# Attention scores as three products of split queries and keys, and the rotary swap of neighbours done by DMA

## The reference, cut to what matters

```python
q = apply_rope(split_heads(x @ Wq))        # pairs (x1, x2) -> (x1*cos - x2*sin, x1*sin + x2*cos)
k = apply_rope(split_heads(x @ Wk))
v = split_heads(x @ Wv)
sim = einsum('bid,bjd->bij', q, k) * d ** -0.5
sim = where(tril, sim, -inf)
out = einsum('bij,bjd->bid', softmax(sim), v) @ Wo + bo
x = layernorm(x + out)                     # then the experts and a second layernorm
```

## Time and profile before

| | |
|---|---|
| median of 3 runs | 835.21 us (835.08 to 835.27) |
| profiled execution: its span, from the first to the last instruction | 833.1 us |
| what lies around the span, against the median | 2.1 us |
| PE / PEld busy | 813.1 / 587.2 us |
| DVE / ACT / POOL busy | 675.5 / 629.0 / 553.9 us |
| granted TensorE clock, mean | 0.997 |
| units 2 to 61, each | 10.19 us without router work on PE, up to 11.0 us with it |

### The profile page before, as it was taken

The page is one execution under the profiler, slowest core; times in us unless marked ns, Lnnn a source line. Parts: engine busy times, 40 slices in busy tenths (PEclk is TensorE's granted clock), DMA queues, the critical chain, the costliest instruction groups (busy, mean ns, idle before and its releaser), DMA issues.

```text
span 833.1 us, 21102 instructions
## 1 busy us (share of the span) xinstructions
PE 813.1 (98%) x6267; PEld 587.2 (70%) x6267; DVE 675.5 (81%) x2711; ACT 629.0 (76%) x1672; POOL 553.9 (66%) x612
## 2 busy tenths in 40 slices
PE   8999999999999999999999999999999989999995
PEld 4556667666666666666666666666666669999994
DVE  6787798889888988898889988988898866224996
ACT  4677787888788878887888788878887766555576
POOL 5765646456756775667568866675677336899893
PEclk9999999999999999999999999999999999999998
DMA  5111101000100010001000100010012257424434
GB/s 164 33 40 39 52 20 33 8 20 27 53 14 26 27 40 14 26 28 39 15 27 26 39 15 27 26 39 15 14 36 72 71 143 205 131 82 127 128 114 155
DMA packets 55438, 46.09 MB, mean 55 GB/s; under 512 B 6368, under 2 KB 47072, under 8 KB 55328
## 3 DMA queue, kind: packets, MB, share of 16 engines
q1 hardware_dynamic: 50960, 35.90, 15.0%
q0 software_dynamic: 4224, 8.72, 3.1%
q10 hardware_dynamic: 144, 0.13, 0.1%
HBM read 28.39 MB, written 12.14 MB: 49 GB/s over the span
## 4 chain that ended last, share of the span: by engine, by line
PE 94%; DVE 3%; issue 1%; ACT 1%; DMA 1%; POOL 0%; SPq 0%; DVEq 0%
PE TB L1026 18%; PE S_all L979 18%; PE TB L1010 14%; PE S_all L1177 7%; PE AO L1047 7%; PE TB L1190 4%; PE AO L1190 4%; PE AO L906 4%; PE S_all L1010 3%; PE AO L908 3%; PE AO L907 3%; PE AO L968 1%; PE AO L970 1%; PE AO L969 1%; PE AO L903 1%
## 5 line engine op out<-in xcount | busy, mean ns | idle before, releaser
L1295 ACT ACTIVATE Pr_all<-Sm,nmax 128x512 f32<-128x512 f32 (+3 forms) x512 | 279.6, 550 | 0.0
L1504 DVE CUSTOM_DVE_ANT_0 Sm<-S_all,causal 128x512 f32<-128x512 f32 (+3 forms) x512 | 220.2, 487 | 70.9 <-PE S_all L979 70.8
L665 POOL TENSOR_TENSOR shared<-shared,sin_t 128x512 f32<-128x512 f32 x63 | 80.3, 1275 | 172.3 <-DVE shared L1484 172.1
L1307 ACT ACTIVATE PT<-TB 128x1024 f32<-128x1024 f32 x185 | 130.9, 742 | 63.8 <-PE TB L1010 62.8
L979 PE MATMUL S_all<-kT,qT 64*128 64x512 f32 (+3 forms) x1024 | 166.7, 443 | 1.9 <-POOL kT L668 0.9
L1026 PE MATMUL TB<-PT,shared 128*64 128x128 f32 x1008 | 152.3, 441 | 2.3 <-ACT PT L1307 0.3
L1525 DVE SCALAR_TENSOR_TENSOR x_acc<-AO,rinv,x_acc 128x128 f32<-128x128 f32 x504 | 141.7, 344 | 3.5 <-PE AO L1047 1.2
L1010 PEld LDWEIGHTS TB<-ident,Pr_all 128*128 128x128 f32 x1000 | 108.0, 141 | 38.3 <-ACT Pr_all L1295 21.1
L1010 PE MATMUL TB<-ident,Pr_all 128*128 128x128 f32 x1000 | 133.8, 277 | 0.5 <-ACT PT L1307 0.5
L979 PEld LDWEIGHTS S_all<-kT,qT 64*128 64x128 f32 x1024 | 78.9, 187 | 71.2 <-issue 54.4
L1026 PEld LDWEIGHTS TB<-PT,shared 128*64 128x64 f32 x1008 | 60.5, 136 | 52.0 <-issue 32.7
(11 more groups left out here) (320 smaller groups left out, 1423.9 us busy)
## 6 DMA issues: line engine op xcount, KB each, us to landing
wo<-in_wo SPq DMA_DIRECT2D x64, 64.0 KB, 1.8
PT<-yrows SPq DMA_DIRECT2D x7, 512.0 KB
w_tile<-in_wup SPq DMA_DIRECT2D x10, 256.0 KB
xt<-xrows SPq DMA_DIRECT2D x32, 65.0 KB
x_acc<-in_x SPq DMA_DIRECT2D x8, 256.0 KB
wdown<-in_wdown SPq DMA_DIRECT2D x8, 256.0 KB, 3.2
pay<-pay SPq DMA_DIRECT2D x8, 256.0 KB
x_acc<-pay SPq DMA_DIRECT2D x8, 256.0 KB
```

Of the source, the lines that this page charges most:

```text
L665: nc.gpsimd.tensor_tensor(k_rot, k_rot, sin_t[:, :], ALU.mult).then_inc(k_mul, 1)
L1295: nc.scalar.activation(Pr[j][:, 0:n], Sm[j], ACT.Exp, bias=nmax[:, j:j + 1], scale=-1.0, accum_out=rsum[p][:, h * QB + qb:h * QB + qb + 1] ...
L1307: last = nc.scalar.activation(PT[p][:, :, 0:qb + 1, qb * P:qb * P + P], source, ACT.Copy)
L1504: nc.vector.tensor_tensor_reduce(out=Sm[j], in0=SB[2 * (group % 2) + h][:, at:at + n], in1=causal[:, T - n:T], scale=-0.125, scalar=HUGE, ...
```

## The change

Three things change, all in the attention.

- **The rotation.** DVE multiplies the projected k by the cosine table and, as it is, by a sine table whose rows are swapped (`sign[::-1]` in `rope_tables`). The swap of neighbours comes after: two DMAs issued by SP write the odd rows of `k_rot` into the even rows of `kT`, and the even into the odd. POOL then adds `k_cos`. The same for q. Units 0 and 1 (`PLAIN`) swap on DVE with the `stream_shuffle` that all units used.
- **The split.** From unit 2 on, ACT copies `kT` into `k_hi` with rounding to float32r and POOL writes `k_lo = kT - k_hi`; the same for the last 384 queries.
- **The scores.** Query blocks 1 to 3 are each the sum of three float32r products, high*high, high*low and low*high. Block 0 (128 keys) stays one float32 product, and is now ahead of block 2 in its group.

`PT` and `Pr` are packed more closely (`pt_written`, `pt_rows`), which makes room in SBUF; the shapes that are copied stay the same. The experts' part is unchanged.

```diff
+PLAIN = 2
+SWAPPED = 2 * 16
@@ SP, at the end of each unit
+                if u + 2 < UNITS:
+                    swap_k(u + 2, p)
+                    swap_q(u + 2, p)
+            def swap_k(u, p):
+                sp.wait_ge(k_read, u + 1)
+                wait(sp, scored, BLK * (u - 1))
+                sp.dma_start(kT[p][0:P:2, :], k_rot[1:P:2, :]).then_inc(k_swapped, 16)
+                sp.dma_start(kT[p][1:P:2, :], k_rot[0:P:2, :]).then_inc(k_swapped, 16)
+            def swap_q(u, p):
+                sp.wait_ge(q_read, u + 1)
+                sp.dma_start(qT[p][0:P:2, :], q_rot[1:P:2, :]).then_inc(q_swapped, 16)
+                sp.dma_start(qT[p][1:P:2, :], q_rot[0:P:2, :]).then_inc(q_swapped, 16)
@@ POOL
             def rotate_k(u, p):
-                pool.wait_ge(k_read, u + 1)
-                nc.gpsimd.tensor_tensor(k_rot, k_rot, sin_t[:, :], ALU.mult).then_inc(k_mul, 1)
-                wait(pool, scored, BLK * (u - 1))
-                pool.wait_ge(k_mul, u + 1)
-                nc.gpsimd.tensor_tensor(kT[p][:, :], k_cos, k_rot, ALU.add).then_inc(k_ready, 1)
+                pool.wait_ge(k_swapped, SWAPPED * (u + 1))
+                nc.gpsimd.tensor_tensor(kT[p][:, :], k_cos, kT[p][:, :], ALU.add).then_inc(k_ready, 1)
+            def split_k(u, p):
+                pool.wait_ge(qk_high, 2 * (u - PLAIN) + 1)
+                nc.gpsimd.tensor_tensor(k_lo[p][:, :], kT[p][:, :], k_hi[p][:, :], ALU.subtract).then_inc(qk_split, 1)
+            def split_q(u, p):
+                pool.wait_ge(qk_high, 2 * (u - PLAIN) + 2)
+                nc.gpsimd.tensor_tensor(q_lo[p][:, :], qT[p][:, P:T], q_hi[p][:, :], ALU.subtract).then_inc(qk_split, 1)
...
                     rotate_k(u + 2, p)
                     rotate_q(u + 2, p)
+                    split_k(u + 2, p)
+                    split_q(u + 2, p)
@@ PE, score(u, p, group)
+                for qb in sorted(GROUPS[group]):
...
+                    for h in range(2):
+                        nc.tensor.matmul(banks[h], q_hi[p][halves[h], rows], k_hi[p][halves[h], 0:n], start=True, stop=False)
+                    for h in range(2):
+                        nc.tensor.matmul(banks[h], q_hi[p][halves[h], rows], k_lo[p][halves[h], 0:n], start=False, stop=False)
+                    for h in range(2):
+                        nc.tensor.matmul(banks[h], q_lo[p][halves[h], rows], k_hi[p][halves[h], 0:n],
+                                         start=False, stop=True).then_inc(scored, 1)
@@ PE, ahead of score(u, p, 0)
-                pe.wait_ge(q_ready, u + 1)
-                pe.wait_ge(k_ready, u + 1)
+                if u < PLAIN:
+                    pe.wait_ge(q_ready, u + 1)
+                    pe.wait_ge(k_ready, u + 1)
+                else:
+                    pe.wait_ge(qk_split, 2 * (u - PLAIN) + 2)
@@ ACT
+            def high_k(u, p):
+                act.wait_ge(k_ready, u + 1)
+                nc.scalar.activation(k_hi[p][:, :], kT[p][:, :], ACT.Copy).then_inc(qk_high, 1)
+            def high_q(u, p):
+                act.wait_ge(q_ready, u + 1)
+                nc.scalar.activation(q_hi[p][:, :], qT[p][:, P:T], ACT.Copy).then_inc(qk_high, 1)
...
+                splits = PLAIN <= u + 1 < UNITS
+                if splits:
+                    high_k(u + 1, 1 - p)
                 if not first:
                     copy_pt(u - 1, 1 - p, 0)
+                if splits:
+                    high_q(u + 1, 1 - p)
@@ DVE, rope_k; rope_q alike
-                nc.vector.stream_shuffle(k_rot, bank[:, :], swap).then_inc(k_read, 1)
+                nc.vector.tensor_tensor(k_rot, bank[:, :], sin_t[:, :], ALU.mult).then_inc(k_read, 1)
+                if u < PLAIN:
+                    dve.wait_ge(k_read, u + 1)
+                    nc.vector.stream_shuffle(kT[u % 2][:, :], k_rot, swap).then_inc(k_swapped, SWAPPED)
```

More of the change, by code:

```diff
@@ L3 @@
 from contextlib import ExitStack
+from itertools import accumulate
 F32 = mybir.dt.float32
@@ L143, in sb, with in_turn @@
             return ctx.enter_context(nc.sbuf_tensor(name, shape, dtype))
+        def in_turn(first, then):
+            with ExitStack() as attention_only:
+                held = [attention_only.enter_context(nc.sbuf_tensor(*of)) for of in first]
+            return held, sb(*then)
         def ps(name, shape=(P, 512)):
@@ L186, in build_block @@
         q_cos, q_rot, k_cos, k_rot = (shared[:, 2 * QB * VS * P + PAIRS * P + i * T:2 * QB * VS * P + PAIRS * P + i * T + T] for i in range(4))
[L187 removed]
+        (PT_all, *k_parts), y_all = in_turn(
+            [("PT_all", [P, 2, 2, PT_BLOCKS, P], F32)] + [(f"k_part{i}", [P, T], F32R) for i in range(3)],
+            ("y_all", [P, 2 * 2 * QB * T], F32))
+        (k_part,), ys_first = in_turn([("k_part3", [P, T], F32R)], ("ys_first", [P, 4, C], F32))
+        k_parts.append(k_part)
+        k_hi, k_lo = k_parts[0:2], k_parts[2:4]
         OT = [sb(f"OT{i}", [P, T]) for i in range(2)]
@@ L190, in build_block @@
         Sm = [Sm_of[qb][:, h, :] for h, qb in ORDER]
-        Pr_all = sb("Pr_all", [P, BLK, T])
-        Pr = [Pr_all[:, i, :] for i in range(BLK)]
+        (Pr_all, *q_parts), f_acc = in_turn(
+            [("Pr_all", [P, 2 * PR_BLOCKS * P], F32)] + [(f"q_part{i}", [P, T - P], F32R) for i in range(4)],
+            ("f_acc", [P, NT, C], F32))
+        q_hi, q_lo = q_parts[0:2], q_parts[2:4]
+        ends = list(accumulate((qb + 1) * P for h, qb in ORDER))
+        Pr = [Pr_all[:, end - (qb + 1) * P:end] for end, (h, qb) in zip(ends, ORDER)]
         nmax = sb("nmax", [P, BLK])
@@ L973, in score @@
             def score(u, p, group):
-                for i, qb in enumerate(GROUPS[group]):
-                    at = 3 * P * i
-                    for h in range(2):
-                        half = slice(D * h, D * h + D)
-                        nc.tensor.matmul(SB[2 * (group % 2) + h][:, at:at + (qb + 1) * P], qT[p][half, qb * P:qb * P + P],
-                                         kT[p][half, 0:(qb + 1) * P], start=True, stop=True).then_inc(scored, 1)
+                for qb in sorted(GROUPS[group]):
+                    at, n = 3 * P * GROUPS[group].index(qb), (qb + 1) * P
+                    banks = [SB[2 * (group % 2) + h][:, at:at + n] for h in range(2)]
+                    halves = [slice(D * h, D * h + D) for h in range(2)]
+                    if qb == 0 or u < PLAIN:
+                        for h in range(2):
+                            nc.tensor.matmul(banks[h], qT[p][halves[h], qb * P:qb * P + P], kT[p][halves[h], 0:n],
+                                             start=True, stop=True).then_inc(scored, 1)
+                        continue
+                    rows = slice(qb * P - P, qb * P)
+                    for h in range(2):
+                        nc.tensor.matmul(banks[h], q_hi[p][halves[h], rows], k_hi[p][halves[h], 0:n], start=True, stop=False)
[4 more added lines that the diff above has]
+                                         start=False, stop=True).then_inc(scored, 1)
             def transpose(u, p, group):
@@ L1306, in copy_pt @@
                         source = (wide(u) if group else TB)[:, :, 3 * P * i:(3 * i + qb + 1) * P].rearrange("k h (b q) -> k h b q", q=P)
-                    last = nc.scalar.activation(PT[p][:, :, 0:qb + 1, qb * P:qb * P + P], source, ACT.Copy)
+                    last = nc.scalar.activation(pt_written(p, qb), source, ACT.Copy)
                 last.then_inc(pt_ready, 1)
```

51 lines of the change are left out of this document (25 added, 26 removed).

## The result

The changed kernel takes 851.74 us (median of 4 runs, 848.72 to 853.78), beside 835.24 us for the kernel before on the same chip (835.08 to 836.95): a ratio of 1.0193 [1.0171, 1.0215], slower by 1.9%. The forecast was 829.1 us.

What follows compares the result with a forecast made beforehand. PE's own work and the equally long loop of transposes, ACT copies and attend were taken to bound it. -12.0 us in common units plus 5.9 at three places gave -6.1: 835.2 to 829.1 us, range 820 to 842.

Steps and rivals of the forecast that it cites:

- Three places where this cover is gone: Unit 2, units 42 to 44 and unit 61, where the swap is not hidden: losses of 5.9 us together.
- The swap: DMA swap plus POOL's add: landing 2.1 us, k ready at S + 2.65, hidden; with 2.9, at 3.45, just hidden.
- The scores: PE's products of blocks 3, 2 and 1: 1.59 us instead of 2.00, saving 0.41 a unit, bounds 0.3 and 0.42.
- the weight loads: Rival: three more loads of 0.187 us a unit stand open on PE, 0.15 slower a unit, 848 us; chance 0.08.
- the 64 rows: Rival: float32r products on 64 rows don't run side by side on PE, 1.2 us x 62, 905 us; chance 0.04.
- The copies on ACT: high_k before ACT's first copy: group 1's transposes at S + 5.30, gain 0.27 us a common unit, 12 us over 60.
- Unit 2: Start of the attention: q's swap, add and high_q end at 27.3, attend 1.5 us late (0 to 3).
- Units 42 to 44: Busy POOL stretch: k ready at S + 5.5 instead of 3.55, cost 2 us (0.5 to 5).
- Unit 61: Swap queued on SP behind two 256 KB weight loads: k at S + 5.9, cost 2.4 us (1 to 4).
- the single places cost more than 10 us: Sign that the prediction is wrong: the three places without cover, put at 5.9 us together, cost over 10.
- the eaten gain: Rival: six more waits between four engines leave a common unit only 0.13 us, sum zero, 835 us; chance 0.15.
- a landing of 3.4: Rival of the swap late in every unit: beyond a 3.0 us landing each 0.1 costs 6 us; 847 us, chance 0.13.

Runs made afterwards that it cites:

- Run 7: Both high copies later on ACT in the changed kernel, POOL's subtractions cut to 8 columns from unit 4 on: 834.27 us, 0.9986 of the kernel before.
- run 2: Changed kernel with the k and q swaps issued ahead of the up-weight loads on SP's queue: 842.10 us, 1.0113 of the kernel before.
- runs 4 and 13: Changed kernel's split scores with the old rotation: 4 as such, 850.42 us; 13 with float32 scores in fourth units and 2, 36, 44 to 46, 60, 834.62 us.
- run 3: Changed kernel's rotation with DMA swap alone, every score a float32 product, no high or low parts: 833.43 us, 1.0001 of the kernel before.

## Why the prediction was wrong

The step that failed is **"Three places where this cover is gone ... Together 5.9"**, and within it two things: the size of the three, and that there are three. The three cost 16.9 us in the trace, and 22 other stretches 8.2. Beneath the second lies a term of "The swap" in which a landing of 2.1 us, at the worst 2.9, stood for all units: in eleven stretches the q swap landed so late, 2.9 to 4.4 us after its issue, that ACT waited for it. In numbers, the forecast for the span was -6.1 us and the attention's end moved by +17.9. Of the 24.0 between them, 4.8 are gain that did not come (7.2 instead of 12), 11.0 the size of the three places, and 8.2 what was not listed.

- *The scores: right in kind, too large in size.* The pairs of block 3 are 0.23 us apart, so 64-row pairs run side by side and the three more weight loads are hidden. The rivals of the weight loads and of the 64 rows fall. But PE reaches the transposes of group 0 only 0.24 us earlier (S + 3.01 instead of 3.25), not 0.41 and below the lower bound of 0.3: the score products save 0.32, and project_out, behind them, takes 0.97 us instead of 0.89. Why it does is open.
- *The copies on ACT: a gain near the forecast, in part by luck.* Predicted were 0.27 us in a common unit, as 0.41 that PE saves less what the k copy holds back; measured are 0.21 (34 stretches), with group 1's transposes at S + 5.37 instead of 5.30. Run 7 shows that the k copy holds back nothing there: without it ahead, the first copy starts at the same S + 4.14. Two errors, a saving too large and a cost that wasn't there, nearly cancelled. At n = 1, where the k copy does count, the unit was to lose 0.19 and lost 0.16. The 12 us were counted over 60 units, and only 34 gained, 7.2 us.
- *The swap in a common unit: right for k, not for q.* The landing is 2.1 in the median, and in the 34 shorter stretches POOL begins to add k by S + 2.5. What I left out is the tail (up to 4.4 us) and that q, which goes last of four DMAs, meets it with little to spare: in unit 38 it was issued at S + 1.0, and with a landing of 2.1 it would have been added by 4.5, ahead of its copy at 5.06; it landed at S + 4.3. SP takes 0.47 to 0.60 us for each issue, up to 1.77, where I had 0.35.
- *Unit 2:* +1.5 predicted, +3.8 measured. ACT waits there 3.5 us at the k copy, ahead of the first transposes' copy, which I had looked for only at the q copy; and from 28.5 to 31.5 us the granted clock is 0.50. In run 2, where it stays at 1.00, the start costs +2.4.
- *Units 42 to 44:* +2 predicted, +6.8 (42 to 45) measured. I followed the queue to "k is ready at 5.5 instead of 3.55"; its add ended at S + 6.5, PE stood 2.35 us and the clock fell, which makes unit 43 3.9 us longer. Of the rest 2.7 us are the late q swaps of units 42 and 45, which the queue on POOL has no part in.
- *Unit 61:* +2.4 predicted, +6.3 measured; k was expected at 5.9 and its add ended at 7.5. Run 2 shows the place to be right and the remedy to be the queue's order.
- *What I did not list:* 8.2 us in 22 other stretches. Nine of them wait for a late q swap, and these make 6.0 of the 8.2. The normalization on POOL makes k late in the third and fourth stretches once the swap is gone (runs 4 and 13); with the swap it shows in fewer of them.

I had named "the single places cost more than 10 us" as what would make the prediction wrong; they cost 16.9. Of the rivals the eaten gain is nearest: its "six more waits between four engines" is what happened, but not evenly in all units, and not only to zero. Two rivals are added up wrongly, which didn't move the forecast: by its own rule of 6 us for each 0.1 us a landing of 3.4 gives 853 us and not 847 (and one of 3.3 gives 847, above the range's 842), and 1.2 us x 62 on 835 give about 910 us and not 905.

Why some q swaps take 3 to 4 us can be read from the traces in part. The changed kernel's trace has 56 packets of 16 KB in the DMA queue q8, which the profile calls an instruction queue, each 0.9 to 1.9 us long. All 18 of the 124 q swap DMAs that took over 2.6 us to land have such a packet that starts between 0.4 us before their issue and 1.6 us after it; of those with none from 0.7 us before to 1.6 us after, none took over 2.6 us. In run 3 the 22 with such a packet took 2.5 to 4.2 us and the 102 others 1.9 to 2.9. Run 2 has two late ones (4.2 and 4.3) whose packet, if any, starts later than 1.6 us. So the two go together; that the packet is what holds the swap up is likely and not shown, as no run moved one.

## What to carry to other kernels

An operation that is wanted late but waits for something uncertain must not stand, on an in-order engine, ahead of one that is wanted now; ask for each new wait what is queued behind it. A mean slack over common units says little when helper engines have crowded stretches: follow each engine's queue through every kind of unit. And a change that pays in most units can be kept if the crowded ones stay with the old way: split scores everywhere cost 2.0% with the old rotation, and with 17 more units in float32 they gain 0.5%.
